# Mixture-of-experts rows stored with their weights applied and added by accumulating gathers, float16 routing tables, and statistics taken four batches ahead

## The chip, the cores and the metric

The kernel runs on one core of one Trainium2 chip. It is written instruction by instruction for five engines: TensorE (PE, matmuls and, beside them, PEld, its weight loads), VectorE (DVE), ScalarE (ACT), GpSimd (POOL) and SyncE (SP, which here only issues DMAs). Engines meet through semaphores. The metric is the device time of one execution in microseconds (us).

## The reference

```python
def _L0_ffn_ref(x, gate_w, w1, b1, w2, b2):        # EMBED_DIM 256, HIDDEN 1024, 8 experts, TOP_K 2
    xt = x.reshape(-1, EMBED_DIM)
    probs = jax.nn.softmax(xt @ gate_w.T, axis=-1)
    top_w, top_i = jax.lax.top_k(probs, TOP_K)
    top_w = top_w / (top_w.sum(axis=-1, keepdims=True) + 1e-09)
    h = jnp.einsum('td,ndh->tnh', xt, w1) + b1
    h = jax.nn.gelu(h, approximate=False)
    out_all = jnp.einsum('tnh,nhd->tnd', h, w2) + b2
    sel = jnp.take_along_axis(out_all, top_i[:, :, None], axis=1)
    return (sel * top_w[:, :, None]).sum(axis=1)

def _L1_attn_ref(x, ...):
    xa = _ln(x, ln1_g, ln1_b)
    xx = _shift(xa)                                # one step back along the sequence
    xk, xv, xr = (xa * m + xx * (1 - m) for m in (time_mix_k, time_mix_v, time_mix_r))
    k, v, r = xk @ att_Wk.T, xv @ att_Wv.T, xr @ att_Wr.T
    x = x + (jax.nn.sigmoid(r) * _wkv(time_decay, time_first, k, v)) @ att_Wo.T
    xc = _ln(x, ln2_g, ln2_b)
    xx2 = _shift(xc)
    xk2, xr2 = (xc * m + xx2 * (1 - m) for m in (cm_k, cm_r))
    kk = jnp.square(jax.nn.relu(xk2 @ ffn_Wk.T))
    return x + jax.nn.sigmoid(xr2 @ ffn_Wr.T) * (kk @ ffn_Wv.T)

# x (16, 256, 256) float32
x = x + decay_attention(_layernorm(x))
x = x + causal_attention(_layernorm(x), ctx_1024)
x = x + _L0_ffn_ref(_layernorm(x))
x = x + _L1_attn_ref(_layernorm(x))
x = x + biased_attention(_layernorm(x), ctx_1024)
x = x + float8_linear(_layernorm(x))
```

## The kernel before

The residual `X` stays in SBUF as 32 tiles of 128 tokens by 256 values from the first step to the last. A batch is one sequence, two tiles; `turns` runs a loop body for the 16 batches. `build` calls one function for each of the six steps. The change is in two of them, `experts_ffn` and `time_channel_mix`.

**Gate stretch of `experts_ffn`.** For each batch VectorE measures mean and variance (`measure`, `layer_norm_stats`), GpSimd takes the inverse root (`inverse_root`), VectorE normalises (`norm`, `layer_norm_apply`) into one of two `XN_s`, SyncE stores these rows to the DRAM table `tokens`, TensorE transposes them (`turn_input`), ScalarE copies them to `xT` (`read_input`), and TensorE multiplies by the gate (`gate_tokens`, 8 matmuls a batch of which each loads 128 token columns and moves 8). There is one `stats`, one `aggr` and one `rstd`; VectorE's turn is norm of batch b+2, measure of batch b+3, copy of the gate's result.

**Routing and tables.** VectorE picks the two largest logits, forms the weights `wt`, counts the tokens of each expert with two matmuls, and gives each pair of token and choice a place in a table of NBLK = 71 blocks of 128 rows, sorted by expert (`place`, `blk`, `row`). The token of each place comes out of TensorE: for each of the 64 columns (two choices, 32 tiles) a one-hot table `at_row` (128 wide) is multiplied by a table `at_blk` (71 wide) that holds the token's number in the column of its block, and all 64 products are summed in `p_y`. The tables are made eight columns at a time, in four buffers:

```python
dve.tensor_tensor(at_row[:, g % 4, :, :], ramp[:, :].unsqueeze(1).broadcast_to([P, 8, P]),
                  flat_row[:, 8 * g:8 * g + 8].unsqueeze(2).broadcast_to([P, 8, P]), ALU.is_equal)
for n in range(8 * g, 8 * g + 8):
    last = dve.tensor_scalar(at_blk[:, g % 4, n % 8, :], ramp[:, 0:NBLK], flat_blk[:, n:n + 1], token[:, n % NT:n % NT + 1],
                             ALU.is_equal, ALU.mult)
```

**Expert loop.** 43 groups, 28 of two blocks and 15 of one. SyncE loads a group's `w1` and `w2` (ring of RING = 4), GpSimd gathers its rows from `tokens` by indirect DMAs (`gx`, four groups ahead), TensorE transposes them, multiplies by `w1` (`p_h`), ScalarE applies gelu, TensorE multiplies by `w2` (`p_y`, which waits for `gy_ready` of the group before), VectorE adds the bias `b2` into `gy`, and ScalarE's queue stores `gy` to the DRAM table `rows_out`. VectorE's `read_rows(j + 1)`, the copy of the next group's transposes, stands before `gy` of group j.

**Mixing stage.** `time_channel_mix` runs 16 turns. GpSimd's `fetch` copies the places of a batch to `which` and gathers four tiles from `rows_out` to `got` (two choices, two tiles), three batches ahead and at the end of its own turn; VectorE's `combine` adds them to `X` with their weights, four dependent products of 256 values, and `measure_x` measures the sum. Then come `roots_x` (GpSimd), `norm_in` (ScalarE), transposes (TensorE, `turn_x`), `xa`, the projections `p_k`, `p_v`, `p_r`, the scans and `mixed_out` on VectorE, and `p_y` on TensorE; the second half takes `zn`, `xc`, `dif`, `mixed2`, the 1024 wide hidden layer `p_h` and `p_kv`. The order on each engine is written out by hand. VectorE's turn has `combine(b + 2)` and `measure_x(b + 2)` between `measured_z` of batch b and `dif` of the channel mix of batch b; TensorE's turn is `p_k` of b+1, `p_y` of b, `p_v` and `p_r` of b+1, values of b-1 around the transposes of `zn`, `turn_x` of b+2, then the receptance and hidden matmuls of b.

## Time and profile before

| what | value |
|---|---|
| median of 3 runs | 2022.05 us (2018.77 to 2024.86) |
| profiled execution, its own time | 2026.54 us |
| its span in the profile | 2024.8 us |
| mean granted clock of TensorE | 0.931 |
| instructions | 40826 |
| PE / PEld busy | 1710.0 us (84%) / 1416.4 us (70%) |
| DVE busy | 1252.0 us (62%) |
| ACT busy | 1121.4 us (55%) |
| POOL busy | 563.3 us (28%) |

The rows below use positions in the span (us from its start). A window's "PEclk" is the granted clock of TensorE, as a share of 2.4 GHz. In the timeline a row is one instruction or a run of equal ones; the square brackets give the idle time of the engine ahead of it and what ended it. The gate stretch lies at 425 to 479 us, routing and tables to 524, the expert loop to about 1043, the mixing stage to about 1545.

### The profile page before, as it was taken

What the parts mean: (1) busy time and instruction counts of PE and PEld (TensorE: products, weight loads), DVE (VectorE), ACT (ScalarE), POOL (GpSimd) and SP (SyncE); (2) the same over time, 40 slices, a digit from 0 to 9 for tenths busy, and PEclk for the clock granted to TensorE, in tenths of its full rate; (3) what the DMA queues carried; (4) which work ended last, traced back from release to release, by engine and by line L of the source; (5) the groups of instructions that cost most, each with busy time, mean ns of one, the idle gap of its engine ahead of it and who ended that gap; (6) DMA issues with size and microseconds to landing.
All of it is one profiled execution on the core that took longest, in us unless ns stands there. A gap on an engine that the chain in (4) does not pass through costs nothing. (4 is left out here: it accounts for less than half of the span.)

```text
span 2024.8 us, 40826 instructions
## 1 busy us (share of the span) xinstructions
PE 1710.0 (84%) x13476; PEld 1416.4 (70%) x13476; DVE 1252.0 (62%) x4322; ACT 1121.4 (55%) x2552; POOL 563.3 (28%) x716
## 2 busy tenths in 40 slices
PE   6677777764699999999955999999978999999964
PEld 5455555554588888889954877777766888888842
DVE  6689999857310101011118899999836988888756
ACT  2299999930122222222325666666636888888855
POOL 3333232221211111101115566666520000000017
PEclk9899999965799999999987999999998999999985
DMA  3100000023556555557940000000010000000002
GB/s 115 46 25 24 19 25 18 2 74 115 169 165 202 174 189 183 180 187 247 326 145 13 20 22 22 22 22 22 11 37 15 23 23 23 23 23 23 2 1 84
DMA packets 102049, 154.68 MB, mean 76 GB/s; under 512 B 5760, under 2 KB 85504, under 8 KB 101088
## 3 DMA queue, kind: packets, MB, share of 16 engines
q1 hardware_dynamic: 85600, 125.25, 18.9%
q0 software_dynamic: 6480, 17.70, 2.9%
q10 hardware_dynamic: 9776, 9.31, 1.3%
q8 instruction: 102, 1.67, 0.3%
q14 instruction: 91, 0.75, 0.1%
HBM read 134.54 MB, written 17.69 MB: 75 GB/s over the span
## 5 line engine op out<-in xcount | busy, mean ns | idle before, releaser
L1851 ACT ACTIVATE moe_hT<-moe_p_h,lane_a 128x256 f32<-128x256 f32 (+1 forms) x344 | 131.5, 433 | 370.5 <-PE moe_p_h L1803 370.4
L1803 PE MATMUL moe_p_h<-moe_gT,moe_w 128*128 128x256 f32 (+1 forms) x1376 | 256.3, 345 | 0.8 <-issue 0.8
L1813 PE MATMUL moe_p_y<-moe_w,moe_hT 128*128 128x256 f32 x1136 | 252.3, 379 | 0.0
L1803 PEld LDWEIGHTS moe_p_h<-moe_gT,moe_w 128*128 128x128 f32 x1376 | 227.8, 192 | 25.7 <-issue 1.2
L1362 ACT ACTIVATE xb_pr<-xb_sc,xb_nmax 128x256 f32<-128x256 f32 x512 | 225.3, 502 | 16.6 <-DVE xb_nmax L1441 16.5
L1813 PEld LDWEIGHTS moe_p_y<-moe_w,moe_hT 128*128 128x128 f32 x1136 | 212.5, 190 | 27.1
L1441 DVE CUSTOM_DVE_ANT_0 xb_sc<-xb_p_s,xb_neg 128x256 f32<-128x256 f32 x512 | 187.2, 420 | 54.5 <-PE xb_p_s L1204 48.2
L852 ACT ACTIVATE xa_pr<-xa_sc,xa_nmax 128x256 f32<-128x256 f32 (+1 forms) x512 | 204.7, 456 | 3.4 <-DVE xa_nmax L934 2.8
L1728 POOL DMA_INDIRECT moe_gx<-moe_tokens,moe_source_i x71 | 67.4, 949 | 460.6 <-PE moe_p_t L1790 400.8
L1981 DVE COPY moe_gT<-moe_p_t 128x512 f32<-128x512 f32 (+1 forms) x43 | 25.7, 598 | 234.7 <-PE moe_p_t L1790 234.7
L1992 DVE TENSOR_TENSOR moe_gy<-moe_p_y,lane_a 128x256 f32<-128x256 f32 x71 | 27.5, 421 | 229.1 <-PE moe_p_y L1813 229.1
L934 DVE CUSTOM_DVE_ANT_0 xa_sc<-xa_p_s,xa_neg 128x256 f32<-128x256 f32 (+1 forms) x512 | 151.7, 352 | 15.3 <-PE xa_p_s L674 13.4
L1216 PE MATMUL xb_p_p<-ident,xb_pr 128*128 128x128 f32 x1024 | 133.9, 274 | 6.1 <-DVE xb_prT L1450 6.1
L686 PE MATMUL xa_p_p<-ident,xa_pr 128*128 128x128 f32 x768 | 118.3, 278 | 14.7 <-DVE xa_prT L943 7.1
L1216 PEld LDWEIGHTS xb_p_p<-ident,xb_pr 128*128 128x128 f32 x1024 | 118.3, 142 | 14.3 <-ACT xb_pr L1362 5.7
L2244 PE MATMUL mix_p_kv<-mix_fv,mix_hid_sq 128*128 128x256 f32 x512 | 115.7, 379 | 1.7 <-ACT mix_hid_sq L2408 1.7
L2293 PE MATMUL mix_p_h<-mix_mixed,mix_fk 128*128 128x256 f32 x512 | 113.6, 380 | 0.0
L686 PEld LDWEIGHTS xa_p_p<-ident,xa_pr 128*128 128x128 f32 x768 | 83.7, 142 | 36.2 <-issue 18.4
L2293 PEld LDWEIGHTS mix_p_h<-mix_mixed,mix_fk 128*128 128x128 f32 x512 | 97.8, 191 | 13.5
L2244 PEld LDWEIGHTS mix_p_kv<-mix_fv,mix_hid_sq 128*128 128x128 f32 x512 | 96.0, 190 | 14.5 <-ACT mix_hid_sq L2408 2.1
L1450 DVE COPY xb_prT<-xb_p_p 128x512 f32<-128x512 f32 x128 | 87.6, 684 | 1.7 <-PE xb_p_p L1216 1.7
L1343 ACT ACTIVATE xb_prT<-xb_p_p 128x512 f32<-128x512 f32 x128 | 75.5, 590 | 7.2 <-PE xb_p_p L1216 4.1
(329 smaller groups left out, 3456.4 us busy)
## 6 DMA issues: line engine op xcount, KB each, us to landing
moe_w<-in_L_ffn_w_dram SPq DMA_DIRECT2D x86, 1024.0 KB
moe_rows_out<-moe_gy ACTq DMA_DIRECT2D x28, 256.0 KB
X<-in_x_dram SPq DMA_DIRECT2D x4, 1024.0 KB, 9.5
xa_ctx<-in_ctx_dram SPq DMA_DIRECT2D x16, 256.0 KB, 3.4
moe_tokens<-moe_XN_s SPq DMA_DIRECT2D x16, 256.0 KB, 2.1
xb_ctx<-in_ctx_dram SPq DMA_DIRECT2D x16, 256.0 KB, 2.9
xb_raw<-in_fside_BxSxS_dram SPq DMA_DIRECT2D x16, 256.0 KB, 3.7
out_dram<-X SPq DMA_DIRECT2D x2, 1280.0 KB, 5.2
```

Of the source, the lines that this page charges most:

```text
L686: last = pe.transpose(p_p[m % 2][:, (e * TB + kt) * P:(e * TB + kt + 1) * P], pr[:, m % RB, e, kt * P:(kt + 1) * P], ident[:, :])
L852: last = act.activation(pr[:, n % RB, e, 0:width], sc[:, n % RB, e, 0:width], ACT.Exp, bias=nmax[:, n % RB, e:e + 1], scale=-1.0)
L934: last = dve.tensor_tensor_reduce(out=sc[:, n % RB, e, 0:keys(t)], in0=scored_in(n, e), in1=neg[:, s, t, 0:keys(t)], scale=1.0, scalar=3e3 ...
L1216: last = pe.transpose(p_p[m % 2][:, (e * TB + kt) * P:(e * TB + kt + 1) * P], pr[:, m % RB, e, kt * P:(kt + 1) * P], ident[:, :])
L1362: last = act.activation(pr[:, n % RB, e, :], sc[:, n % RB, e, :], ACT.Exp, bias=nmax[:, n % RB, e:e + 1], scale=-1.0)
L1441: last = dve.tensor_tensor_reduce(out=sc[:, n % RB, e, :], in0=scored_in(n, e), in1=neg[:, s, t, :], scale=1.0, scalar=3e38, op0=ALU.add, ...
L1450: dve.tensor_copy(*turned_unit(m)).then_inc(s_["p_copied_v"], 1)
L1803: last = pe.matmul(p_h[n % 3][:, k * width:(k + 1) * width], w1[:, r, ic, (2 * n + k) * P:(2 * n + k + 1) * P], gT[:, r % 2, ic, 0:width], ...
L1813: last = pe.matmul(p_y[:, t * D:(t + 1) * D], hT[:, hc, t * P:(t + 1) * P], w2[:, r, hc, :], start=(hc == 0), stop=(hc == HC - 1))
L1851: last = act.activation(hT[:, 2 * n + k, 0:width], p_h[n % 3][:, k * width:(k + 1) * width], ACT.Gelu, bias=b1[:, bass.ds(e * HC + 2 * n + ...
L2244: last = pe.matmul(p_kv[:, t * D:(t + 1) * D], hid_sq[:, hc, t * P:(t + 1) * P], fv[:, hc, :], start=(hc == 0), stop=(hc == HC - 1))
L2293: last = pe.matmul(p_h[m % 2][:, k * S:(k + 1) * S], fk[:, ic, (2 * m + k) * P:(2 * m + k + 1) * P], mixed2[:, 0, ic, :], start=(ic == 0), ...
```

## The change

The statistics get a second set (`stats`, `aggr`, `rstd`) and are taken four batches ahead, behind the copy of the gate's result. TensorE gets `keep_busy(2)` twice a turn in the gate stretch: matmuls of a constant bfloat16 tile into a PSUM bank that is free then. The tables are compared in float16 from float16 copies, `at_blk` for eight columns in one instruction and then multiplied by the token's number in another; the two choices come out in separate halves of `p_y`, so that the choice of a place is known too. The weights' arithmetic moves behind the first `read_rows`; SyncE stores the weights to a DRAM table as 8192 single floats, GpSimd gathers one float per row for each group (`draw_weights`), and VectorE scales the bias and then stores `p_y * weight + b2 * weight`. In the mixing stage `which`, `got` and `combine` are gone: gathers with an adding DMA write straight into `X`, the first choice's four batches ahead, the second's three ahead after the first's have landed, and `measure_x` waits for the second's.

```diff
+                if isinstance(j, int) and j == RING - 1:
+                    sp.wait_ge(s_["weights_ready"], 1)
+                    with nc.allow_non_contiguous_dma(reason="one weight per token and choice"):
+                        sp.dma_start(weights.rearrange("(k t p) a -> p (k t a)", k=2, p=P), wt[:, :, :].rearrange("p k t -> p (k t)")).then_inc(s_["loaded_back"], 16)
...
+            pool.memset(warm[:, :], 1.0).then_inc(s_["warm_set"], 1)
+
+            def norm_root(n, s):
+                wait_alone(pool, s_["stood_p"], (s_["measured"], n + 1))
+                inverse_root(pool, rstd[:, s, :], aggr[:, s, :, 1], 1.0, LN_EPS, minus_half[:, :], s_["var_eps"], s_["rstd_ready"], n, s_["stood_p"])
+
+            for n in range(4):
...
             chain.done(pool.tensor_scalar(falling[:, :], ramp[:, 0:E], -1.0, float(E), ALU.mult, ALU.add))
             chain.done(pool.tensor_scalar(steps[:, :], ramp[:, 0:MAXB], float(P), None, ALU.mult))
             chain.done(pool.tensor_scalar(token[:, :], token[:, :], -float(MID), None, ALU.add))
+            chain.done(pool.tensor_copy(ramp_h[:, :], ramp[:, :]))
+            chain.wait()
+            chain.done(pool.tensor_scalar(token_up[:, :], token[:, :], 0.0, None, ALU.is_ge))
...
-                    wait_alone(pool, s_["stood_p"], (s_["measured"], b + 4))
-                    inverse_root(pool, rstd[:, :], aggr[:, :, 1], 1.0, LN_EPS, minus_half[:, :], s_["var_eps"], s_["rstd_ready"], b + 3, s_["stood_p"])
+                if has_next(b, 4):
+                    norm_root(b + 4, s)
...
+            def draw_weights(j):
+
+                if j >= RING:
+                    pool.wait_ge(s_["gy_ready"], j - RING + 1)
+                for t in range(tiles(j)):
+                    n = first_row(j) // P + t
+                    pool.indirect_dma_start(weight[:, j % RING, t:t + 1], None, weights,
+                                            bass.IndirectOffsetOnAxis(ap=weight_i[:, n:n + 1], axis=0)).then_inc(weighed[j % RING], 16)
...
+                if j == RING - 1:
+                    pool.wait_ge(s_["places_ready"], 1)
+                    pool.wait_ge(s_["loaded_back"], 16)
+                    for i in range(RING):
+                        draw_weights(i)
+                elif j >= RING:
+                    draw_weights(j)
...
+            def keep_busy(n):
+
+                for _ in range(n):
+                    pe.matmul(p_c[:, :], warm[:, 0:P], warm[:, :], start=True, stop=True)
...
             for b, h, s in turns(pe, ahead=3):
                 if has_next(b, 2):
                     turn_input(b + 2, s)
+                keep_busy(2)
                 if has_next(b):
                     gate_tokens(b + 1, 1 - s)
+                keep_busy(2)
...
+                    k, at = divmod(8 * g + n, NT)
+                    last = pe.matmul(p_y[:, k * NBLK:(k + 1) * NBLK], at_row[:, g % 4, n, :], at_blk[:, g % 4, n, :],
+                                     start=(at == 0), stop=(at == NT - 1))
...
-            measure(2)
+            measure(2, 0)
+            measure(3, 1)
...
             for b, h, s in turns(dve, ahead=3):
                 if has_next(b, 2):
                     norm(b + 2, s, h + 1)
-                if has_next(b, 3):
-                    measure(b + 3)
                 dve.wait_ge(s_["logits"], b + 1)
                 dve.tensor_copy(lg[:, bass.ds(TB * b, TB), :], p_h[s][:, 0:TB * E].rearrange("p (t e) -> p t e", t=TB)).then_inc(s_["lg_read"], 1)
+                if has_next(b, 4):
+                    measure(b + 4, s)
...
-            flat_row, flat_blk = flat(row[:, :, :]), flat(blk[:, :, :])
+            chain.done(dve.tensor_copy(blk_h[:, :], flat(blk[:, :, :])))
+            step(dve.tensor_copy(row_h[:, :], flat(row[:, :, :])))
             for g in range(2 * NT // 8):
+                own = slice(8 * g, 8 * g + 8)
+                of = slice(8 * g % NT, 8 * g % NT + 8)
                 if g >= 4:
                     dve.wait_ge(s_["hot_read"], g - 3)
-                dve.tensor_tensor(at_row[:, g % 4, :, :], ramp[:, :].unsqueeze(1).broadcast_to([P, 8, P]),
-                                  flat_row[:, 8 * g:8 * g + 8].unsqueeze(2).broadcast_to([P, 8, P]), ALU.is_equal)
-                for n in range(8 * g, 8 * g + 8):
-                    last = dve.tensor_scalar(at_blk[:, g % 4, n % 8, :], ramp[:, 0:NBLK], flat_blk[:, n:n + 1], token[:, n % NT:n % NT + 1],
-                                             ALU.is_equal, ALU.mult)
-                last.then_inc(s_["hot"], 1)
-            chain.done(dve.tensor_copy(place_i[:, :, :], place[:, :, :]))
-            dve.wait_ge(s_["hot_read"], 2 * NT // 8)
-            dve.tensor_scalar(source_i[:, :], p_y[:, 0:NBLK], float(MID), None, ALU.add).then_inc(s_["source_ready"], 1)
-            chain.close()
-
+                chain.done(dve.tensor_tensor(at_blk[:, g % 4, :, :], ramp_h[:, 0:NBLK].unsqueeze(1).broadcast_to([P, 8, NBLK]),
+                                             blk_h[:, own].unsqueeze(2).broadcast_to([P, 8, NBLK]), ALU.is_equal))
+                chain.done(dve.tensor_tensor(at_row[:, g % 4, :, :], ramp_h[:, :].unsqueeze(1).broadcast_to([P, 8, P]),
+                                             row_h[:, own].unsqueeze(2).broadcast_to([P, 8, P]), ALU.is_equal))
+                chain.wait()
+                dve.tensor_tensor(at_blk[:, g % 4, :, :], at_blk[:, g % 4, :, :],
+                                  token_h[:, of].unsqueeze(2).broadcast_to([P, 8, NBLK]), ALU.mult).then_inc(s_["hot"], 1)
...
+            dve.wait_ge(s_["hot_read"], 2 * NT // 8)
+            step(dve.tensor_copy(codes[:, :, :], p_y[:, 0:2 * NBLK].rearrange("p (k n) -> p k n", k=2)))
+            step(dve.tensor_tensor(code[:, :], codes[:, 0, :], codes[:, 1, :], ALU.add))
+            step(dve.tensor_scalar(code_up[:, :], code[:, :], 0.0, -1.0, ALU.is_gt, ALU.mult))
+            step(dve.scalar_tensor_tensor(source[:, :], code[:, :], float(MID), code_up[:, :], ALU.add, ALU.add))
+            dve.tensor_copy(source_i[:, :], source[:, :]).then_inc(s_["source_ready"], 1)
+            step(dve.tensor_scalar(code_up[:, :], codes[:, 1, :], 0.0, float(B * S), ALU.not_equal, ALU.mult))
+            dve.tensor_tensor(weight_i[:, :], source[:, :], code_up[:, :], ALU.add).then_inc(s_["places_ready"], 1)
             read_rows(0, 0)
+            dve.wait_ge(s_["exp_ready"], 1)
+            step(dve.tensor_reduce(zsum[:, :], probs[:, :, :], AX.X, ALU.add))
+            step(dve.reciprocal(wt[:, 0, :], zsum[:, :]))
+            step(dve.tensor_tensor(wt[:, 1, :], gap[:, :], wt[:, 0, :], ALU.mult))
+            step(dve.tensor_tensor(wsum[:, :], wt[:, 0, :], wt[:, 1, :], ALU.add))
+            step(dve.tensor_scalar(wsum[:, :], wsum[:, :], 1e-9, None, ALU.add))
+            step(dve.reciprocal(wsum[:, :], wsum[:, :]))
+            for k in range(2):
+                chain.done(dve.tensor_tensor(wt[:, k, :], wt[:, k, :], wsum[:, :], ALU.mult))
+            chain.done(dve.tensor_copy(place_i[:, :, :], place[:, :, :]))
+            chain.wait()
+            dve.sem_inc(s_["weights_ready"], 1)
+            chain.close()
+
             for j, r, i in groups(dve):
                 e = expert_of(dve, j)
                 if not isinstance(j, int) or j < NG - 1:
                     read_rows(j + 1, (r + 1) % RING)
+                dve.wait_ge(weighed[r], drawn_by(j, r, i))
+                for t in range(tiles(j)):
+                    last = dve.tensor_scalar(b2_w[:, r % 2, t, :], b2[:, bass.ds(e, 1), :].rearrange("p a d -> p (a d)"), weight[:, r, t:t + 1], None, ALU.mult)
+                last.then_inc(s_["bias_ready"], 1)
+                dve.wait_ge(s_["bias_ready"], j + 1)
...
-                    last = dve.tensor_tensor(gy[:, r % 2, t, :], p_y[:, t * D:(t + 1) * D], b2[:, bass.ds(e, 1), :].rearrange("p a d -> p (a d)"), ALU.add)
+                    last = dve.scalar_tensor_tensor(gy[:, r % 2, t, :], p_y[:, t * D:(t + 1) * D], weight[:, r, t:t + 1], b2_w[:, r % 2, t, :], ALU.mult, ALU.add)
...
-            def fetch(n, s):
-
-                if since(n, 2):
-                    wait_alone(pool, s_["stood_p"], (s_["combined"], n - 1))
-                pool.tensor_copy(which[:, s, :, :], place_i[:, :, bass.ds(TB * n, TB)]).then_inc(s_["which_ready"], 1)
-                wait_alone(pool, s_["stood_p"], (s_["which_ready"], n + 1))
-                for k in range(2):
-                    for t in range(TB):
-                        pool.indirect_dma_start(got[:, s, k, t, :], None, rows_out,
-                                                bass.IndirectOffsetOnAxis(ap=which[:, s, k, t:t + 1], axis=0)).then_inc(fetched[s], 16)
+            def fetch(n, k):
+
+                if k == 1:
+                    pool.wait_ge(fetched[0][n % 2], 32 * (n // 2) + 32)
+                for t in range(TB):
+                    pool.indirect_dma_start(tile_of(X, n, t), None, rows_out,
+                                            bass.IndirectOffsetOnAxis(ap=place_i[:, k, TB * n + t:TB * n + t + 1], axis=0),
+                                            compute_op=ALU.add).then_inc(fetched[k][n % 2], 16)
...
-            fetch(1, 1)
+            fetch(1, 0)
...
+            fetch(0, 1)
+            fetch(1, 1)
...
             fetch(2, 0)
+            fetch(3, 0)
+            fetch(2, 1)
...
+                if has_next(b, 4):
+                    fetch(b + 4, 0)
                 if has_next(b, 3):
-                    fetch(b + 3, 1 - s)
+                    fetch(b + 3, 1)
...
-                dve.wait_ge(fetched[s], 64 * h + 64)
-                for k in range(2):
-                    for t in range(TB):
-                        last = dve.scalar_tensor_tensor(tile_of(X, n, t), got[:, s, k, t, :], wt[:, k, bass.ds(TB * n + t, 1)],
-                                                        tile_of(X, n, t), ALU.mult, ALU.add)
...
             def measure_x(n):
+                dve.wait_ge(fetched[1][n % 2], 32 * (n // 2) + 32)
```

## Rows read from the trace of the kernel before

**Rows 1.** windows: PE, PEld, DVE, ACT, POOL busy (x instructions), PEclk, DMA share, GB/s
```profile
50.00:60.00 10.00, 8.48 (x52) 7.30 (x51) 9.21 (x27) 2.71 (x6) 4.45 (x9) 1.00 0.00 1
...
425.00:479.00 54.00, 42.11 (x192) 40.33 (x192) 27.47 (x111) 9.55 (x16) 16.50 (x44) 0.50 0.30 103
...
550.00:1000.00 450.00, 450.00 (x2302) 400.69 (x2301) 46.47 (x99) 113.91 (x292) 54.79 (x58) 1.00 0.62 204
...
1130.00:1430.00 300.00, 274.64 (x1284) 232.71 (x1284) 277.15 (x484) 187.99 (x356) 192.58 (x184) 1.00 0.07 20
```
**Rows 2.** timeline of the gate stretch: start, us busy, engine, line, group [idle before, releaser]
```profile
440.83 0.73 DVE L91 TENSOR_SCALAR moe_XN_s<-X,moe_aggr,moe_rstd 128x256 f32<-128x256 f32 x2 [1.24 <-POOL moe_rstd L85]
...
441.62 0.71 PEld L1744 LDWEIGHTS moe_p_t<-ident,moe_XN_s 128*128 128x128 f32 x4 [0.45 <-DVE moe_XN_s L91]
...
442.32 1.83 PEld L1753 LDWEIGHTS moe_p_h<-lane_a,moe_xT 128*128 128x128 f32 x8
...
443.81 0.73 DVE L91 TENSOR_SCALAR moe_XN_s<-X,moe_aggr,moe_rstd 128x256 f32<-128x256 f32 x2 [1.24 <-POOL moe_rstd L85]
```
**Rows 3.** timeline of two earlier stages, at clock 1.00
```profile
60.98 0.97 PEld L304 LDWEIGHTS dec_p_m<-dec_ones,dec_osq 128*128 128x128 f32 x8 [0.97 <-DVE dec_o L379]
...
113.75 0.60 PE L640 MATMUL xa_p_a<-lane_b,xa_cT 128*128 128x256 bf16 x4
```
**Rows 4.** groups of instructions by form, whole run: busy, mean ns | idle before
```profile
L640 PE MATMUL xa_p_a<-lane_b,xa_oT 128*128 128x256 bf16 x64 | 9.8, 275 | 11.4 <-ACT xa_oT L800 11.4
...
L965 DVE TENSOR_TENSOR xa_y_f<-xa_y_r,xa_rows_d 128x256 bf16<-128x256 bf16 x32 | 7.9, 288 | 10.4 <-ACT xa_y_r L824 10.3
```
**Rows 5.** timeline of the routing and the tables
```profile
485.75 1.06 PE L1769 MATMUL moe_p_t<-moe_both,moe_ones 128*128 128x256 f32 x2
...
487.88 0.42 DVE L1927 COPY moe_total<-moe_p_t 128x256 f32<-128x256 f32 x1
...
507.86 1.22 DVE L1967 TENSOR_TENSOR moe_at_row<-moe_ramp,moe_row 128x1024 f16<-128x1024 f32 x1
...
510.81 1.22 DVE L1967 TENSOR_TENSOR moe_at_row<-moe_ramp,moe_row 128x1024 f16<-128x1024 f32 x1
```
**Rows 6.** timeline of the expert loop's first groups
```profile
529.45 0.69 DVE L1981 COPY moe_gT<-moe_p_t 128x512 f32<-128x512 f32 x1 [5.81 <-PE moe_p_t L1790]
...
546.84 5.34 PE L1803 MATMUL moe_p_h<-moe_gT,moe_w 128*128 128x256 f32 x24
```
**Rows 7.** parts 3 and 6 of the page: queues, and one of the DMA issues
```profile
q1 hardware_dynamic: 85600, 125.25, 18.9%
...
q10 hardware_dynamic: 9776, 9.31, 1.3%
...
moe_tokens<-moe_XN_s SPq DMA_DIRECT2D x16, 256.0 KB, 2.1
```
**Rows 8.** timeline of one full turn of the mixing stage
```profile
1273.27 1.59 PEld L2232 LDWEIGHTS mix_p_y<-lane_b,mix_mixed_out 128*128 128x128 f32 x8 [1.32 <-DVE mix_mixed_out L2512]
...
1275.59 0.94 POOL L2156 DMA_INDIRECT mix_got<-moe_rows_out,mix_which  x1 [0.30 <-issue]
...
1278.31 2.84 DVE L2431 SCALAR_TENSOR_TENSOR X<-mix_got,wt,X 128x256 f32<-128x256 f32 x4 [0.51 <-DMA mix_got<-moe_rows_out,mix_which]
...
1285.07 0.67 DVE L2552 TENSOR_TENSOR mix_dif<-mix_xc 128x512 f32<-128x512 f32 x1
...
1296.62 1.59 PEld L2220 LDWEIGHTS mix_p_k<-mix_mixed,lane_b 128*128 128x128 f32 x8 [0.26 <-DVE mix_mixed L2423]
...
1299.53 1.59 PEld L2232 LDWEIGHTS mix_p_y<-lane_b,mix_mixed_out 128*128 128x128 f32 x8 [1.32 <-DVE mix_mixed_out L2512]
```
**Rows 9.** timeline of turn 14 of the mixing stage
```profile
1457.39 1.59 PEld L2232 LDWEIGHTS mix_p_y<-lane_b,mix_mixed_out 128*128 128x128 f32 x8 [1.32 <-DVE mix_mixed_out L2512]
...
1467.82 0.69 DVE L2552 TENSOR_TENSOR mix_dif<-mix_xc 128x512 f32<-128x512 f32 x1 [1.51 <-ACT mix_xc L2388]
```
**Rows 10.** timeline of the mixing stage's head
```profile
1055.38 1.80 DVE L2431 SCALAR_TENSOR_TENSOR X<-mix_got,wt,X 128x256 f32<-128x256 f32 x4 [10.11 <-DMA mix_got<-moe_rows_out,mix_which]
```

77 lines of the change are left out of this document (37 added, 40 removed).

## The prediction

> **What bounds the kernel now.** I read the stages first (busy time by window), then the timeline of each stage that the diff touches, then the queues. Four stretches matter, and each has another limit.
>
> In the gate stretch (425 to 479 us) the granted clock of TensorE is 0.50, its 1.2 GHz level [rows 1], and no engine is full. The reader is to see the loop in [rows 2]: `layer_norm_apply` starts at 440.83 and its next turn at 443.81, after 1.24 us of idle that GpSimd's root ends. One batch takes 2.97 us because normalise, measure and root share one `aggr` and one `rstd` and follow each other. VectorE itself has 27.47/16 = 1.72 us of work a batch [rows 1], TensorE 0.71 us of transposes and 1.83 us of gate loads [rows 2].
>
> From 479 to 523.65 us VectorE runs one chain of small steps. The one-hot tables take eight turns of 510.81 - 507.86 = 2.95 us, 23.6 us in all [rows 5].
>
> In the expert loop (550 to 1000) TensorE is busy 450.00 of 450.00 us at clock 1.00 [rows 1]. What the other engines do there costs nothing unless TensorE must wait for it.
>
> In the mixing stage VectorE has 277.15 of 300 us [rows 1]. One turn, from one `p_y` load to the next, is 1299.53 - 1273.27 = 26.26 us [rows 8], and TensorE waits in it: 0.26 us before `p_k` for VectorE's mix and 1.32 us before `p_y` for `mixed_out`. VectorE's wait in the turn is 0.51 us for the gathered rows, before `combine`, which then takes 2.84 us; everything from the first lost half microsecond on is one block of about 3.4 us.
>
> **The change, part by part.**
>
> *Gate stretch.* `measure` now runs four batches ahead with two copies of `aggr` and `rstd`, so the root leaves the loop. VectorE's turn falls to about 1.85 us (its 1.72 and the gaps). TensorE gets four warm matmuls of 512 bf16 columns a batch. A 256-column one costs (0.60 - 0.275)/3 = 0.108 us at the 2.4 GHz level [rows 3, 4], so four of 512 cost 8 x 0.108 = 0.87 us, and 1.73 us at 1.2 GHz. At 2.4 GHz eight loads of 128 columns with hardly any moving columns take 0.97 us [rows 3]; the transposes lie between half of 0.71 and 0.71, I take 0.54. A batch is then 0.54 + 0.97 + 0.87 = 2.4 us at the high level and 0.71 + 1.83 + 1.73 = 4.27 us at the low one. TensorE becomes the limit either way. Which level? Before, TensorE was busy with short loads and stayed at 0.50 [rows 1]. The first stage of the kernel has transposes and matmuls in bursts with gaps, at TensorE busy 8.48 of 10 us, and holds 1.00 [rows 1]; the new loop has no gaps, so I take the high level from the third turn on. The norm at 440.83 is the fifth batch's, so the third's is at 434.9 and the last's at 473.5. These 13 turns take 38.6 us now; with two cold and eleven warm ones they take 8.5 + 26.4 = 34.9: -3.7. Behind the last norm 5.5 us remain until the stretch ends at 479; at the high level transposes, copy, gates and warm matmuls there take about 3.2: -2.3. And the third norm starts some 2 us sooner, since three measurements and roots are done ahead of it. Together -8.0 us; one or three cold turns make it -10 or -6. The `warm` memset lies on GpSimd ahead of the first measurement, the two more set-up copies and two more adds behind the fourth root; both are done long before the fifth root is needed, so nothing. The token stores on SP's queue keep their order.
>
> *Tables.* Per group of eight columns, one 1024-wide compare and eight 71-wide instructions become one 568-wide compare, the 1024-wide one, a wait, and a 568-wide multiply. At one element a cycle, which is what 1.22 us for 1024 says, 568 elements take 0.59 + 0.075 us when the next instruction follows at once and the waited-on compare 1.26: 0.67 + 1.26 + 0.67 = 2.60 us. Eight groups: 20.8 against 23.6, -2.8 us. Two float16 copies of 64 columns add 0.3. Behind the last matmul one write of 71 columns becomes five steps (copy of 142 columns, add, compare, add, cast) of about 0.25 us, as small steps go beside the 0.42 for 256 columns at 487.88 [rows 5]: +1.0. The weights' arithmetic moves away, but the counts land at 485.75 + 1.06 = 486.8 and the copy that needs them starts at 487.88 [rows 5], so only -1.0 of it was on the path. Sum -2.5 us. If float16 ran two elements a cycle the group would be 0.37 + 0.72 + 0.37 = 1.46 us and the tables -11.9; a dense bfloat16 add nearly does, 0.288 us for 256 columns [rows 4]. I take one a cycle: no row has a 16-bit operand that repeats one element. The Trainium skill speaks here against the gain: "Vector Engine (DVE) Microarchitecture Reference", § 5.1, gives the paired mode only to operands that step by one element and reports one repeated element at the single rate, and every compare and multiply here has such an operand. By that rule -2.8 stands, by the dense row -11.9.
>
> *Weights out and back.* SP waits for `weights_ready` behind the fourth load, stores 8192 single floats at a stride of 128, and GpSimd waits for the landing before it draws four groups of weights; behind that wait stand the fifth gather of rows (TensorE wants it four groups of 14 us later) and, on VectorE, `gy` of group 0. The arithmetic sits in front of `read_rows(1)`, where VectorE idles, behind the copy that starts at 529.45 [rows 6]; with its 0.69 and 2.7 for ten small steps it ends at 532.8. Landing after T us, two draws of 1.25 each and 1.8 until they land (1276.54 to 1278.31, [rows 8]), then bias and `gy` 1.6: done at 538.7 + T. TensorE wants `gy` of group 0 when `p_y` of group 1 begins: 24 of its 32 hidden matmuls take 5.34 us from 546.84 on, all 32 take 7.1, and four transposes follow, 0.6 at this clock: 554.5 [rows 6]. So T up to 16 us is free and every further microsecond stalls TensorE. No row has 4-byte writes. Bounds: a whole 256 KB token store lands in 2.1 us [rows 7]; by the mean packet of queue q10 (1.3% of 16 x 2024.8 us over 9776 packets = 43 ns for 0.95 KB) 8192 of them on 16 engines take 22 us, by q1's 71.5 ns for 1.46 KB 37 us [rows 7]. I take 19, just under q10, whose packet is the smaller: +3, bounds 0 and +21. The Trainium skill has a price by "VectorE: DVE Perf Modes", § The three transpose paths: a strided DMA transpose takes 19 times 1309 ns; for half of its 16,384 elements that is, as an estimate, 12.4 us, by which this term would be 0.
>
> In the rest of that loop each pair of tiles adds two draws (2.5 us on GpSimd) and two bias products (0.8 us on VectorE) to engines that are idle most of 14 us; `gy` stays one instruction a tile. Without cover it would be 3.3 us a group; with TensorE at 450 of 450 it is nothing.
>
> *Mixing stage.* `combine` and `which` go; four accumulating gathers a turn replace four plain ones. VectorE's block of 3.4 us does not come back whole. Turn 14 has no `combine` and shows what is late next: there `dif2` starts 1467.82 - 1457.39 = 10.43 us after `p_y`, behind 1.51 us of idle for `xc` [rows 9], against 1285.07 - 1273.27 = 11.80 in a full turn [rows 8]. So VectorE's loop shrinks by 1.37: 10.43 + (1299.53 - 1285.07 = 14.46) = 24.89 us. TensorE's own loop is 26.26 - 1.32 - 0.26 = 24.68: its waits for `zn` and `yn` hang on ScalarE, behind the same `xc`, and stay. The turn is 24.9 us. GpSimd sets the third loop. Its four gathers end at 1276.54 (1275.59 + 0.94 [rows 8]) and VectorE is released 1.8 us later, at 1278.31. Without `which` and its 0.82 us wait the rows land at 5.6 us of the turn; VectorE has room until 6.5 before `dif2` slips. An excess e over a plain gather (landing plus four times the issue) is free up to about 1, and from 2 on it sets the turn: two turns are 48.7 + e, 24.35 + e/2 each. Bounds of e: 0, and 5.6 if both issue (0.95 each) and landing (1.8) double, a turn of 27.1. I take e = 2, since an accumulating gather moves the same rows once more: 25.35 by the strict loop, 24.9 if the contended copies on VectorE shrink as in turn 14; I take 25.0, -1.26 a turn. That counts in turns 1 to 13. Turn 0 doesn't wait for `combine`: 0. 13 x 1.26 = -16.4 us.
>
> At the stage's head VectorE waits 10.11 us for four gathers and has 1.80 us of `combine` before it measures [rows 10]. Now two gathers must land before two more are issued: -1.8 for `combine`, -1.2 for `which` and its wait, about +3 for the second round (issue and landing once more): 0, bounds -4 and +3. The stages before 425 and after the mixing stage are untouched.
>
> **Sum.** -8.0 - 2.5 + 3 + 0 - 16.4 = -23.9, about -24 us on the profiled execution's 2026.5 (span 2024.8 and 1.7 around it): 2002.5. That execution is 4.5 us above the median of the runs, 2022.05; against the median I predict 1998 us. Some 0.3% (6 us) is what a measurement of this kernel can tell from no change.
>
> **Rivals.**
> 1. *The float16 tables run at the paired rate:* -9 more, 1989. For: the dense row. Against: the repeated operand. 0.08.
> 2. *The clock stays low in the gate stretch.* Then a turn is 4.27 instead of 2.97: +18 instead of -8, 2024, no change. For: gate loads hardly move columns, and the same stretch sat at 0.50 while 78% busy. 0.12.
> 3. *The single-float store is slow,* as by q1: +21 instead of +3, 2016. For: a packet's time hardly falls with its size between q1 and q10. Against: four bytes are far less than either moves. 0.10.
> 4. *The turn of the mixing stage doesn't shorten,* since another loop binds (ScalarE, or contention that moves with the work): 2014. For: TensorE's own loop is only 1.58 us shorter than the turn now. Against: turn 14 shows every other step going faster. The leaving of `combine` would then do nothing. 0.10.
> 5. *Slower: the accumulating gathers.* For: two of a batch's gathers wait for the other two. Against: the rows land at 5.6 where 6.5 would do. Place: GpSimd's end of each turn. The rest gives -7.5, so the turn must be above 26.26 + 13.5/13 = 27.3, e above 5.9, or 1 us more issue each and 2 us of landing. With e = 9 a turn is 28.85: +34 - 7.5, 2048. 0.07.
> My forecast: 0.53, own range 1988 to 2009.
>
> The cases between 2016 and 2028 are most of 2 and half of 3; above lie 5 and what is left of 2. Faster 0.77, same 0.13, slower 0.10. For 8 in 10 the range runs from the paired rate with small gains, 1980, to 2020.
>
> **What the profile will show.** Gate stretch: clock 1.00 from about 440 and a turn of 2.4 us, or 0.50 and 4.3. Tables: 568-wide instructions of 0.75 us, a group at 2.6. `gy` of group 0 before 554 less the 10 us gained, and no TensorE gap there. Mixing: `dif2` waits for `xc` in every turn, `p_y` to `p_y` 24.9 to 25.3, VectorE waiting less than 1.5 us for rows. Wrong would be my forecast above all if accumulating gathers hold GpSimd longer than 0.95 us each, or if the clock doesn't rise.

## The result, and the profile after

The changed kernel takes 2017.28 us (median of 14 executions, 2013.83 to 2024.11) against 2022.16 us for the kernel before (14 executions). The ratio is 0.9977 with a 95% interval of 0.9967 to 0.9986: a gain of 4.6 us where 24 were forecast. Measured once more it was 0.9997 (0.9982 to 1.0011), so the gain is near the bound of what can be told from nothing.

The profiled execution of the changed kernel took 2013.83 us (span 2012.0) and is the fastest of its 14. That matters for every difference below: it is 12.7 us under the profiled execution of before, while the medians are 4.9 us apart. So I put the second profile of the changed kernel (from the control experiment, after_again) beside it. The bounds of the stages are the first or last start of one instruction: first statistics of the gate stretch, last copy of gate results, the write of `source_i`, the last `gy`, the first statistics of `X` in the mixing stage, the first and the last `mixed_out`. All in us.

| stage | before | after | after, second profile | forecast | measured |
|---|---|---|---|---|---|
| up to the gate stretch | 425.5 | 423.3 | 425.3 | 0 | -2.2 / -0.2 |
| gate stretch | 53.5 | 42.1 | 42.1 | -8.0 | -11.4 / -11.4 |
| routing and tables | 44.4 | 41.8 | 41.6 | -2.5 | -2.6 / -2.8 |
| expert loop | 516.8 | 530.2 | 536.1 | +3 | +13.4 / +19.3 |
| head, to the first statistics | 17.1 | 21.8 | 21.4 | 0 | +4.7 / +4.3 |
| from there to the first `mixed_out` | 27.8 | 28.3 | 28.4 | 0 | +0.5 / +0.6 |
| turns of the mixing stage | 393.1 | 380.6 | 381.7 | -16.4 | -12.5 / -11.4 |
| rest | 546.6 | 543.9 | 545.1 | 0 | -2.7 / -1.5 |
| span | 2024.8 | 2012.0 | 2021.7 | -23.9 | -12.8 / -3.1 |

The two stages that the change doesn't touch, the first and the last, differ by up to 2.7 us between these three executions (by 3.4 and 5.4 us over all fourteen profiles of this document), nearly as much as the whole gain of the medians; a changed stage's own difference is what can be read.

**Gate stretch.** Windows of the changed kernel (columns as in [rows 1]):

```profile
430.00:460.00 30.00, 29.27 (x196) 24.36 (x201) 22.43 (x88) 7.35 (x13) 15.97 (x42) 0.88 0.32 106
```

The timeline from the moment at which the clock is up:

```profile
440.89 1.08 PEld L1805 LDWEIGHTS moe_p_h<-lane_a,moe_xT 128*128 128x128 f32 x8
441.07 0.74 DVE L91 TENSOR_SCALAR moe_XN_s<-X,moe_aggr,moe_rstd 128x256 f32<-128x256 f32 x2
...
442.67 0.21 PEld L1812 LDWEIGHTS moe_p_c<-moe_warm 128*128 128x128 bf16 x2
442.78 0.59 PE L1812 MATMUL moe_p_c<-moe_warm 128*128 128x512 bf16 x2
...
443.19 0.74 DVE L91 TENSOR_SCALAR moe_XN_s<-X,moe_aggr,moe_rstd 128x256 f32<-128x256 f32 x2
```

Against [rows 2] the turn is 443.19 - 441.07 = 2.12 us in place of 2.97, the normalising instruction has no idle time ahead of it, and the eight gate loads take 1.08 us in place of 1.83, at granted clock 1.00. One wait for the root is left, once, near the stretch's start; GpSimd's set-up stands before that root, with the four small steps that the change adds to it:

```profile
436.88 0.74 DVE L91 TENSOR_SCALAR moe_XN_s<-X,moe_aggr,moe_rstd 128x256 f32<-128x256 f32 x2 [1.37 <-POOL moe_rstd L85]
```

**Tables.** The timeline of one group:

```profile
489.81 0.74 DVE L2016 TENSOR_TENSOR moe_at_blk<-moe_ramp_h,moe_blk_h 128x568 f16<-128x568 f16 x1
...
490.47 1.22 DVE L2018 TENSOR_TENSOR moe_at_row<-moe_ramp_h,moe_row_h 128x1024 f16<-128x1024 f16 x1
...
491.72 0.75 DVE L2021 TENSOR_TENSOR moe_at_blk<-moe_at_blk,moe_token_h 128x568 f16<-128x568 f16 x1
...
492.39 0.74 DVE L2016 TENSOR_TENSOR moe_at_blk<-moe_ramp_h,moe_blk_h 128x568 f16<-128x568 f16 x1
```

A group takes 492.39 - 489.81 = 2.58 us (2.60 forecast, 2.95 before). The 1024-wide compare costs 1.22 us with float16 inputs as it did with float32 inputs [rows 5].

**The weights, out and back.** The timeline around the second group of the expert loop:

```profile
516.19 0.37 SPq L1714 DMA_DIRECT2D moe_weights<-wt  x1
...
523.88 7.07 PE L1868 MATMUL moe_p_y<-moe_w,moe_hT 128*128 128x256 f32 x32
...
541.03 0.94 POOL L1765 DMA_INDIRECT moe_weight<-moe_weights,moe_weight_i  x1 [23.32 <-DMA moe_weights<-wt]
...
548.07 0.61 DVE L2057 TENSOR_SCALAR moe_b_w<-lane_a,moe_weight 128x256 f32 x2 [23.30 <-DMA moe_weight<-moe_weights,moe_weight_i]
...
548.72 0.88 DVE L2064 SCALAR_TENSOR_TENSOR moe_gy<-moe_p_y,moe_weight,moe_b_w 128x256 f32<-128x256 f32 x2
...
549.65 8.87 PE L1868 MATMUL moe_p_y<-moe_w,moe_hT 128*128 128x256 f32 x32 [11.35 <-DVE moe_gy L2064]
```

This is the main line of the document. SyncE issues the store at 516.19, GpSimd's first draw leaves at 541.03, its row reaches VectorE at 548.07, and TensorE, whose 32 matmuls of the second group wait for `gy` of the first, stands idle for 11.35 us. When it starts its granted clock has fallen to 0.50 (window 545 to 548 us), and the 32 matmuls take 8.87 us and not 7.07 as a group earlier, 1.8 us more. 11.35 + 1.8 = 13.2 of the stage's 13.4 us. The list of DMA issues has the store itself, with its size and the time to landing:

```profile
moe_weights<-wt SPq DMA_DIRECT2D x1, 32.0 KB, 24.1
```

The same view's row for queue q1 shows the pieces, 93808 packets where [rows 7] has 85600; 8192 of the 8208 more are the floats:

```profile
q1 hardware_dynamic: 93808, 125.28, 20.1%
```

In the second profile of the same kernel the landing took 29.3 us and TensorE's gap 15.7 us.

**Mixing stage.** The head (timeline):

```profile
1041.56 1.60 POOL L2223 DMA_INDIRECT X<-moe_rows_out,place_i  x1 [31.20 <-POOLq L144]
...
1047.15 1.53 POOL L2223 DMA_INDIRECT X<-moe_rows_out,place_i  x1 [0.31 <-issue]
...
1053.41 1.54 POOL L2223 DMA_INDIRECT X<-moe_rows_out,place_i  x1 [4.49 <-DMA X<-moe_rows_out,place_i]
...
1059.15 0.75 DVE L2503 BATCH_NORM_STATS2 mix_stats<-X 128x6 f32<-128x256 f32 x2 [16.53 <-DMA X<-moe_rows_out,place_i]
```

VectorE waits 16.53 us where [rows 10] has 10.11 and 1.80 of `combine`. A full turn:

```profile
1269.94 1.59 PEld L2306 LDWEIGHTS mix_p_y<-lane_b,mix_mixed_out 128*128 128x128 f32 x8 [0.51 <-DVE mix_mixed_out L2576]
...
1271.04 1.54 POOL L2223 DMA_INDIRECT X<-moe_rows_out,place_i  x1 [0.30 <-issue]
...
1272.89 1.54 POOL L2223 DMA_INDIRECT X<-moe_rows_out,place_i  x1 [0.30 <-issue]
...
1276.72 0.75 DVE L2503 BATCH_NORM_STATS2 mix_stats<-X 128x6 f32<-128x256 f32 x2 [2.25 <-DMA X<-moe_rows_out,place_i]
...
1280.86 0.67 DVE L2613 TENSOR_TENSOR mix_dif<-mix_xc 128x512 f32<-128x512 f32 x1
...
1289.21 4.66 DVE L2497 SCALAR_TENSOR_TENSOR mix_mixed<-mix_dif,lane_b,mix_xa 128x256 f32<-128x256 f32 x6
1289.53 1.46 POOL L2216 TENSOR_TENSOR X<-X,mix_g 128x512 f32<-128x512 f32 x1
...
1295.27 1.59 PEld L2306 LDWEIGHTS mix_p_y<-lane_b,mix_mixed_out 128*128 128x128 f32 x8 [0.52 <-DVE mix_mixed_out L2576]
```

From `p_y` to `p_y` it is 25.33 us (26.26 in [rows 8]). The wait for rows has grown from 0.51 to 2.25 us, an accumulating gather holds GpSimd for 1.54 us where a plain one took 0.94, and TensorE waits 0.52 us for `mixed_out` where it waited 1.32. `dif` comes 10.92 us after `p_y`; from `dif` to the next `p_y` are 14.41 us.

### The profile page after: what moved, and what is told of

Read it like the earlier page. It is cut to its first block and busy times, and to the rows that moved or that the text cites. A ratio compares the mean times of both kernels' runs of the same rounds, so it can differ in the third digit from the quotient of the medians.

```text
span 2012.0 us, 40950 instructions
## 1 busy us (share of the span) xinstructions
PE 1700.0 (84%) x13535; PEld 1404.7 (70%) x13540; DVE 1240.9 (62%) x4289; ACT 1121.0 (56%) x2552; POOL 649.8 (32%) x776
## 3 DMA queue, kind: packets, MB, share of 16 engines
q1 hardware_dynamic: 93808, 125.28, 20.1%
## 5 line engine op out<-in xcount | busy, mean ns | idle before, releaser
L1868 PE MATMUL moe_p_y<-moe_w,moe_hT 128*128 128x256 f32 x1136 | 254.1, 381 | 11.4 <-DVE moe_gy L2064 11.4
L1858 PEld LDWEIGHTS moe_p_h<-moe_gT,moe_w 128*128 128x128 f32 x1376 | 227.9, 192 | 25.8 <-issue 1.2
L1868 PEld LDWEIGHTS moe_p_y<-moe_w,moe_hT 128*128 128x128 f32 x1136 | 213.8, 191 | 39.1 <-DVE moe_gy L2064 11.6
L1765 POOL DMA_INDIRECT moe_weight<-moe_weights,moe_weight_i x71 | 67.0, 943 | 347.0 <-DVE moe_gy L2064 301.7
L934 DVE CUSTOM_DVE_ANT_0 xa_sc<-xa_p_s,xa_neg 128x256 f32<-128x256 f32 (+1 forms) x512 | 151.7, 352 | 15.3 <-PE xa_p_s L674 13.4
L2064 DVE SCALAR_TENSOR_TENSOR moe_gy<-moe_p_y,moe_weight,moe_b_w 128x256 f32<-128x256 f32 x71 | 31.8, 480 | 204.2 <-issue 129.0
L2223 POOL DMA_INDIRECT X<-moe_rows_out,place_i x64 | 101.2, 1581 | 52.7 <-POOLq L144 31.2
```

Of the source, the lines that this page charges most:

```text
L934: last = dve.tensor_tensor_reduce(out=sc[:, n % RB, e, 0:keys(t)], in0=scored_in(n, e), in1=neg[:, s, t, 0:keys(t)], scale=1.0, scalar=3e3 ...
L1858: last = pe.matmul(p_h[n % 3][:, k * width:(k + 1) * width], w1[:, r, ic, (2 * n + k) * P:(2 * n + k + 1) * P], gT[:, r % 2, ic, 0:width], ...
L1868: last = pe.matmul(p_y[:, t * D:(t + 1) * D], hT[:, hc, t * P:(t + 1) * P], w2[:, r, hc, :], start=(hc == 0), stop=(hc == HC - 1))
L2223: pool.indirect_dma_start(tile_of(X, n, t), None, rows_out, bass.IndirectOffsetOnAxis(ap=place_i[:, k, TB * n + t:TB * n + t + 1], axis=0) ...
```

## The experiments

Twelve kernels ran, the last of them the changed kernel itself. Those whose expectation names the changed kernel are built on it, and their ratios too are to the kernel before, so they are to be held against 0.9977; two ratios whose intervals overlap are not told apart. Because the executions differ as the table shows, I read each one's stage in its profile first and its ratio second.

### Which part of the gate stretch's edit gives the gain

`gate_both` is the kernel before with the statistics and the warm matmuls of the change, and nothing else:

```diff
-            for b in range(3):
-                wait_alone(pool, s_["stood_p"], (s_["measured"], b + 1))
+            pool.memset(warm[:, :], 1.0).then_inc(s_["warm_set"], 1)
+            for n in range(4):
+                norm_root(n, n % 2)
...
+                keep_busy(2)
                 if has_next(b):
                     gate_tokens(b + 1, 1 - s)
+                keep_busy(2)
```

> The kernel before with the gate stretch alone changed: two sets of statistics taken four batches ahead, and the warm matmuls. My theory after reading the two traces: the whole 13.6 us that the gate's last copy comes earlier (479.01 to 465.38) belong to this edit, so the kernel takes 2022 - 13.6 = 2008.5 us, ratio 0.993, with turns of 2.1 us at granted clock 1.00. Rival: part of it is given back later in the stage, because weight loads of the first experts or the routing then wait; then the ratio is above 0.995.

Ratio 0.9947 (0.993 to 0.9964), 2014.28 us: 10.7 us gained. Its gate stretch took 41.9 us, 11.6 less than before, and no later stage is more than 0.8 us longer (expert loop 517.5): nothing is given back. The 13.6 us of the theory had 2.2 us in them by which that execution of the changed kernel reached the stretch earlier. gate_both is faster than the whole change, by intervals that don't overlap.

`gate_ahead` leaves out `warm` and both `keep_busy(2)`:

```diff
-                keep_busy(2)
                 if has_next(b):
                     gate_tokens(b + 1, 1 - s)
-                keep_busy(2)
```

> The kernel before with the statistics four batches ahead, without warm matmuls. Theory A: the clock needs the warm matmuls, so TensorE stays at 0.50 and its own 0.71 + 1.83 us and what it waits for ScalarE's copy set a turn of 2.6 to 2.8 us against 2.97: -3 to -5 us, ratio 0.998. Theory B: losing the root's wait is enough to raise the clock; then turns fall below 2 us and the gain is -14 or more, ratio 0.993.

Ratio 0.9956 (0.9941 to 0.9971), 8.9 us gained, stretch 44.4 us, 9.1 less than before. Neither theory was right: the clock stayed at 0.50, as A said, but the gain was twice to three times what A allowed. That the warm matmuls bring the other 1.8 us of gate_both isn't shown, as the two intervals overlap. Timeline:

```profile
449.39 0.90 PEld L1745 LDWEIGHTS moe_p_t<-ident,moe_XN_s 128*128 128x128 f32 x4
...
450.28 1.83 PEld L1754 LDWEIGHTS moe_p_h<-lane_a,moe_xT 128*128 128x128 f32 x8
...
451.85 0.90 PEld L1745 LDWEIGHTS moe_p_t<-ident,moe_XN_s 128*128 128x128 f32 x4
```

The turn is 2.46 us: TensorE's loads back to back at granted clock 0.50, the 1.2 GHz level, with no wait in them.

`gate_warm` is the kernel before with the warm matmuls and the old statistics:

```diff
+                keep_busy(2)
                 if has_next(b):
                     gate_tokens(b + 1, 1 - s)
+                keep_busy(2)
```

> The kernel before with the warm matmuls, statistics as before. If the 2.97 us loop of measure, root and normalise is what binds, the clock rises but the turn stays near 2.97 us: 0 to -3 us, ratio 0.9985 to 1. If TensorE's low clock was in the loop, the turn falls to about 2.4: -8 us, ratio 0.996.

Ratio 0.9986 (0.9975 to 0.9997), inside the first of the two forecasts, but the stretch itself took 55.1 us in its profile, 1.6 more than before, so the little that the ratio shows isn't shown to come from there. The windows show why the stretch is no shorter (columns as in [rows 1]):

```profile
450.00:455.00 5.00, 4.77 (x21) 4.10 (x22) 1.82 (x7) 0.60 (x1) 1.58 (x3) 0.50 0.23 74
455.00:460.00 5.00, 5.00 (x27) 3.78 (x27) 2.68 (x11) 0.62 (x2) 0.89 (x2) 0.66 0.15 52
460.00:465.00 5.00, 4.95 (x39) 4.27 (x39) 2.83 (x13) 1.77 (x3) 1.53 (x4) 1.00 0.31 107
```

Until the clock rose, at about 458, four matmuls of 512 columns a turn at the low level made turns of 4.1 us out of 2.97. In the ten profiles with both edits the clock rose between 437 and 446 us, and the stretch took 41.7 to 45.7 us accordingly: each turn at the low level costs 2 us more than one at the high level. A window of the changed kernel, and two of second_first, in which it rose last:

```profile
434.00:438.00 4.00, 4.00 (x20) 2.98 (x21) 1.93 (x9) 0.60 (x1) 2.96 (x9) 0.62 0.16 52
```

```profile
442.00:446.00 4.00, 4.00 (x18) 3.10 (x17) 1.78 (x7) 0.60 (x1) 0.93 (x2) 0.50 0.18 60
446.00:450.00 4.00, 3.93 (x31) 3.30 (x31) 2.94 (x13) 0.90 (x2) 0.93 (x2) 1.00 0.31 104
```

### Why the store of the weights is slow

`packed_weights` lays the table out by partition, so that a partition stores its 64 floats in one piece, and gets the place from three more small steps:

```diff
-                        sp.dma_start(weights.rearrange("(k t p) a -> p (k t a)", k=2, p=P), wt[:, :, :].rearrange("p k t -> p (k t)")).then_inc(s_["loaded_back"], 16)
+                        sp.dma_start(weights.rearrange("(p k t) a -> p (k t a)", k=2, p=P), wt[:, :, :].rearrange("p k t -> p (k t)")).then_inc(s_["loaded_back"], 16)
...
-            step(dve.tensor_scalar(code_up[:, :], codes[:, 1, :], 0.0, float(B * S), ALU.not_equal, ALU.mult))
-            dve.tensor_tensor(weight_i[:, :], source[:, :], code_up[:, :], ALU.add)
+            step(dve.tensor_scalar(code_up[:, :], codes[:, 1, :], 0.0, float(NT), ALU.not_equal, ALU.mult))
+            step(dve.scalar_tensor_tensor(code[:, :], source[:, :], float(2 * NT), code_up[:, :], ALU.mult, ALU.add))
+            step(dve.tensor_scalar(code_up[:, :], source[:, :], 1.0 / P, -0.498, ALU.mult, ALU.add))
+            step(dve.tensor_scalar(code_up[:, :], code_up[:, :], ROUND, -ROUND, ALU.add, ALU.add))
+            dve.scalar_tensor_tensor(weight_i[:, :], code_up[:, :], 1.0 - 2 * NT * P, code[:, :], ALU.mult, ALU.add)
```

> The changed kernel with the table of weights laid out by partition: each partition stores its 64 floats as one piece of 256 bytes, and three more small VectorE steps work out the place. Theory: the 24.8 us from the store's issue to the first draw are 8192 pieces of 4 bytes, so they fall to 2 or 3 us, TensorE's 11.4 us gap before the second group's second matmuls and the 1.8 us of low clock behind it go: -13 us against the changed kernel, about 2004 us, ratio 0.991. Rival: the store waits for the expert weights' loads on the same queue; then the landing stays near 24 us whatever the pieces' size, and the ratio stays 0.998. Second rival: the draws, which land 7 us after their issue, hold VectorE anyway; then about half of the gap stays.

Ratio 0.9884 (0.9864 to 0.9903), 2002.05 us. The DMA issue and the timeline:

```profile
moe_weights<-wt SPq DMA_DIRECT2D x1, 32.0 KB, 2.3
```

```profile
521.03 0.34 SPq L1714 DMA_DIRECT2D moe_weights<-wt  x1
...
524.08 0.95 POOL L1765 DMA_INDIRECT moe_weight<-moe_weights,moe_weight_i  x1 [1.49 <-DMA moe_weights<-wt]
...
535.58 0.88 DVE L2067 SCALAR_TENSOR_TENSOR moe_gy<-moe_p_y,moe_weight,moe_b_w 128x256 f32<-128x256 f32 x2 [5.78 <-PE moe_p_y L1868]
```

The same 32 KB on the same queue behind the same loads land in 2.3 us. `gy` waits for TensorE and no longer the other way round, and the expert loop takes 516.5 us as before. The rival (waiting behind the experts' loads) and the second rival (the draws) fall. The edit changes the number of the pieces and their addresses together (64 neighbouring floats a partition for floats 128 apart); no run parts the two. Against the changed kernel the ratio is about 19 us better, more than the 13.4 of its fastest execution's profile and near the 19.3 of the second: the landing of the 8192 pieces took 23.9 to 29.3 us in the six profiles that have it, and the loop 529.9 to 536.1 us.

### What sets the turn of the mixing stage

`second_first` swaps two issues at the end of GpSimd's turn:

```diff
+                if has_next(b, 3):
+                    fetch(b + 3, 1)
                 if has_next(b, 4):
                     fetch(b + 4, 0)
-                if has_next(b, 3):
-                    fetch(b + 3, 1)
```

> The changed kernel with the order of two issues on GpSimd swapped in the mixing stage: the second choice's gathers of batch b+3 ahead of the first choice's of b+4. Theory: in the changed kernel a turn is 25.34 us because the second choice's rows land 2.25 us after VectorE has begun to wait; they are issued 3.7 us sooner here, the wait goes, and the turn falls to 24.7 to 24.9, where TensorE's own work or ScalarE's copy xc binds: -0.5 us in 12 turns, -6 us against the changed kernel. Rival: the turn is held by something that only looks like the wait (ScalarE or shared ports); then the idle time moves elsewhere and the turn stays within 0.1 of 25.34.

Ratio 0.998 (0.9971 to 0.999). My theory fell. The wait for rows is gone from VectorE, as meant, and the turn is 25.34 us all the same:

```profile
1275.46 1.59 PEld L2306 LDWEIGHTS mix_p_y<-lane_b,mix_mixed_out 128*128 128x128 f32 x8 [0.53 <-DVE mix_mixed_out L2576]
...
1279.90 0.74 DVE L2503 BATCH_NORM_STATS2 mix_stats<-X 128x6 f32<-128x256 f32 x2
...
1285.89 0.69 DVE L2613 TENSOR_TENSOR mix_dif<-mix_xc 128x512 f32<-128x512 f32 x1 [1.03 <-ACT mix_xc L2462]
...
1294.66 4.73 DVE L2497 SCALAR_TENSOR_TENSOR mix_mixed<-mix_dif,lane_b,mix_xa 128x256 f32<-128x256 f32 x6
1295.05 1.46 POOL L2216 TENSOR_TENSOR X<-X,mix_g 128x512 f32<-128x512 f32 x1
...
1300.81 1.59 PEld L2306 LDWEIGHTS mix_p_y<-lane_b,mix_mixed_out 128*128 128x128 f32 x8 [0.53 <-DVE mix_mixed_out L2576]
```

So the accumulating gathers, dear as they are, did not hold the turn: `dif` starts 10.43 us after `p_y`, as in [rows 9], and the next `p_y` follows 14.92 us later. What is long is this second half of VectorE's turn. Its six products for the time mix take 4.73 us, and GpSimd's two additions to `X` lie beside them. In the kernel before they took 3.48 us:

```profile
1294.66 3.48 DVE L2423 SCALAR_TENSOR_TENSOR mix_mixed<-mix_dif,lane_b,mix_xa 128x256 f32<-128x256 f32 x6
```

The groups of instructions from 1130 to 1430 us, first of the kernel before and then of the changed one, give the mean of one product:

```profile
L2423 DVE SCALAR_TENSOR_TENSOR mix_mixed<-mix_dif,lane_b,mix_xa 128x256 f32<-128x256 f32 x72 | 42.0, 647 | 0.0
```

```profile
L2497 DVE SCALAR_TENSOR_TENSOR mix_mixed<-mix_dif,lane_b,mix_xa 128x256 f32<-128x256 f32 x72 | 56.7, 851 | 0.0
```

`gathers_first` has the swap of `second_first` and also moves GpSimd's two additions behind the gathers:

```diff
-                if not first(b):
-                    add_g(b - 1)
-                if not ended(b):
-                    add_y(b)
                 if has_next(b, 3):
                     fetch(b + 3, 1)
                 if has_next(b, 4):
                     fetch(b + 4, 0)
+                if not first(b):
+                    add_g(b - 1)
+                if not ended(b):
+                    add_y(b)
```

> The kernel of second_first with one more move on GpSimd: its two additions to X (512 columns each, two inputs) stand behind the four gathers instead of ahead of them. With the rows early the turn stayed at 25.34 us, so the wait for them was not what held it. Theory: VectorE's six products for the time mix now run beside these two additions and take 4.7 us instead of 3.5, which is where the rest of the expected gain went. Here they run beside gathers, which only issue: 3.5 us again, and the turn falls to 24.3 to 24.8 us, -6 to -10 us. Rival A: the additions then meet VectorE's adds of Y and the statistics 3 us later and only move the loss: turn 25.2 to 25.5. Rival B: the products' time depends on the gathers' traffic, not on the additions: then they stay at 4.7 us.

The same group in gathers_first, in the same window:

```profile
L2497 DVE SCALAR_TENSOR_TENSOR mix_mixed<-mix_dif,lane_b,mix_xa 128x256 f32<-128x256 f32 x72 | 32.3, 513 | 0.0
```

851 ns (853 in second_first) fell to 513, the six to 2.70 us, beside gathers instead of additions: rival B is out. The turn, from `p_y` to `p_y`, became 24.95 us:

```profile
1250.17 1.70 PEld L2306 LDWEIGHTS mix_p_y<-lane_b,mix_mixed_out 128*128 128x128 f32 x8
...
1275.11 1.70 PEld L2306 LDWEIGHTS mix_p_y<-lane_b,mix_mixed_out 128*128 128x128 f32 x8
```

That is neither the 24.3 to 24.8 of the theory nor the 25.2 to 25.5 of rival A. `p_y` waits no more for `mixed_out`, and TensorE has only 1.41 us of idle left in the turn, for `yn`; its own loop is longer than I had put it. The turns of the stage took 376.9 us in place of 380.6, 3.7 us less. The ratio, 0.9978 (0.9964 to 0.9992), doesn't show it, and its interval is too wide to: 3.7 us are 0.0018.

`plain_rows` keeps the weighted rows and goes back to plain gathers and additions by VectorE:

```diff
+            def combine(n, s, h):
+                dve.wait_ge(fetched[s], 64 * h + 64)
+                for k in range(2):
+                    for t in range(TB):
+                        last = dve.tensor_tensor(tile_of(X, n, t), got[:, s, k, t, :], tile_of(X, n, t), ALU.add)
```

> The changed kernel with the rows still stored weighted, but gathered plainly into a buffer in the mixing stage as before and added to X by VectorE (tensor_tensor in place of scalar_tensor_tensor). Theory: the gain of the mixing turns, 0.9 us each, comes from VectorE being rid of the four additions, so the turn goes back to 26.2 or 26.3 and the head of the stage gets back its shorter 13.9 us; against the changed kernel +12 for the turns, -4.5 for the head: +7 us. Rival: the turn was shortened by something else (the weights' scalar operand, or buffers); then it stays at 25.3. The gathers' issue must fall from 1.55 to 0.95 us each if adding is what makes them dear.

Ratio 1.0003 (0.9991 to 1.0016), 5 us above the changed kernel. Turns are back at 26.1 to 26.5 us (391.5 us for all, against 380.6), the head at 17.1 (against 21.8), a gather's issue between 0.94 and 1.30 us. So the accumulating gathers, with the additions that they take off VectorE, bring 10.9 us in the turns and cost 4.7 in the head.

### The head of the mixing stage

`loads_late` puts one wait ahead of SyncE's three loads:

```diff
+            sp.wait_ge(fetched[1][0], 32)
             sp.dma_start(fk[:, :, :], ins["pack_fk"].rearrange("p (c h) -> p c h", c=DC))
```

> The changed kernel with SyncE's three loads at the head of the mixing stage (3.3 MB) held until the first batch's gathers of the first choice have landed. Theory: these loads are what makes the first gathers land 8 us after their issue and the head 4.5 us longer than before; then the first measurement comes 18.3 us after the stage's start now and at about 12 us here, -6 us, unless fk and fv come too late for the hidden layer. Rival: two rounds of gathers with 1.55 us issues are by themselves 12 to 13 us long, and little moves: under 2 us.

The wait in the kernel is for the second choice's gathers of the first batch, not the first choice's, so the loads left even later than the expectation says, at 1057.89 us. The head took 18.0 us against 21.8 and nothing later waited (28.3 us to the first `mixed_out`, as in the changed kernel): -3.8 us, between theory and rival. Ratio 0.9954 (0.9936 to 0.9972), which overlaps that of the changed kernel, so only the stage shows it. The loads explain most of the 4.7 us; with 18.0 the head is within a microsecond of the 17.1 of before.

### Together

`all_three` has the edits of packed_weights, second_first and loads_late.

> The changed kernel with the table of weights laid out by partition, the second choice's gathers issued first, and the three loads held at the stage's head. If the parts are independent: -13 (weights), -6 (order), -6 to 0 (head) against the changed kernel's 2017: 1992 to 1998 us, ratio 0.985 to 0.988. If the head's loads matter the other way (fk or fv late), 2003.

Ratio 0.987 (0.9853 to 0.9886), 1997.38 us: 27 us under the kernel before. The parts add up except the swap, which by itself was worth nothing.

`all_four` adds the move of gathers_first.

> The kernel of all_three (weights by partition, second choice's gathers first, loads held) with GpSimd's two additions behind the gathers. By the theory of gathers_first 1997.4 - 6 to 10 = 1988 to 1991 us, ratio 0.983; by rival A 1997, ratio 0.987.

Ratio 0.9864 (0.9841 to 0.9886), 1996.32 us. Its turns took 377.7 us (380.6 in all_three) but its gate stretch 45.7 (42.3). The two can't be told apart by their times.

`four_no_warm` takes both `keep_busy(2)` out of it.

> The kernel of all_four without the warm matmuls in the gate stretch (statistics still four batches ahead). With them the stretch took 41.7 to 45.7 us from execution to execution, as the granted clock rose earlier or later; without them (gate_ahead) 44.4 us. Theory: the warm matmuls are worth nothing to 2 us on average: ratio 0.986 to 0.988, the stretch 44.4 us, and the spread of the times narrower. Rival: they also raise the clock of what follows (routing, first experts), then 3 us or more are lost, ratio 0.989.

Ratio 0.9868 (0.9841 to 0.9896), 1994.69 us: the warm matmuls are worth nothing that can be measured. The granted clock was 0.50 from 430 to 470 us. The stretch took 45.7 us, not the 44.4 of gate_ahead, because of one wait of TensorE, which is 0.47 us long there:

```profile
438.06 0.71 PEld L1796 LDWEIGHTS moe_p_t<-ident,moe_XN_s 128*128 128x128 f32 x4 [1.83 <-DVE moe_XN_s L91]
```

It waits for VectorE, and VectorE for the root behind GpSimd's set-up, which in gate_ahead is four small steps shorter. Whether the times spread less isn't settled: four times lie within 5.7 us (1993.58 to 1999.31) where the four of all_four lie within 7.2; the five of gate_ahead lie within 2.2 us and the six of gate_both within 9.0, but the kernel before, without warm matmuls too, spread over 8.1 us in the 16 times beside those.

`after_again` is the changed kernel itself.

> The changed kernel once more on this chip, as the measure for the other runs: ratio 0.997 to 0.999; the gap of 11 to 12 us before the second group's second matmuls, mixing turns of 25.34 us and a head of 21.5 to 22 us must come back in its trace, while the gate stretch may lie anywhere from 41.7 to 45.7 us.

Ratio 0.9997 (0.9982 to 1.0011), turns of 25.31 to 25.35 us, head 21.4 us, gate stretch 42.1 us. The ratio lies above the 0.997 to 0.999 that I expected, the head 0.1 us under its range, and the gap of TensorE was 15.7 us, outside the 11 to 12 that I expected to come back.

## Why the prediction was right or wrong

The direction was right, as far as 4.6 us can be told from nothing, and the size wrong by a factor of five, 24 us forecast. The steps that failed are the weights' way out and back, put at +3 us and measured at +13.4 and +19.3, then the mixing stage's head, put at 0 and measured at +5, and its turns, 4 to 5 us short of the gain; the gate stretch brought 3.4 us more than its term. By its own steps:

- **Gate stretch, -8.0: -11.4 in two profiles, -7.8 to -11.8 over the ten with both edits.** The likeliest clock came true. The turn was 2.12 us for the 2.4 of the sum. What the prediction had not seen is that the high clock matters little: with the root out of the loop and no warm matmuls a turn at the low clock is 2.46 us (gate_ahead), and 8.9 of the 10.7 us come that way. Rival 2 was priced rightly, 4.27 us a turn at the low level and 4.1 measured, and every execution pays it in two to four turns before the clock rises. Two smaller things were wrong. The turns were laid back from 440.83 at an even 2.97 us, which puts the third norm at 434.9; it is at 433.84 in the trace, because the turn from 433.84 to 437.86 is 4.0 us long, with 2.23 us of wait for the root behind GpSimd's set-up. And the longer set-up is not "done long before the fifth root is needed": that norm still waits 1.37 us. Beside TensorE's long turns at the low level this costs nothing; in four_no_warm it costs 1.3 us.
- **Tables, -2.5: -2.6 and -2.8.** A group took 2.58 us for the 2.60 worked out. The single rate was right and rival 1 is out: float16 inputs gain nothing, 1.22 us for 1024 elements as with float32. By the Trainium skill, "Vector Engine (DVE) Microarchitecture Reference", § 5.1, a two-source operation with 2-byte operands, one of which repeats one element, ran at the single rate, and the trace agrees.
- **Weights out and back, +3: +13.4 and +19.3.** This is the step that failed most. The mechanism was put rightly, with its place (`gy` of group 0 against `p_y` of group 1), and so was the bound, 0 to +21. Three sizes were off. The landing was put at 19 us, below the 22 of q10's packet, though the rows gave no packet under 43 ns; it took 24.1 to 29.3. Group 0's two draws were given 2.5 + 1.8 = 4.3 us from the first issue to the landing, by the gathers of the mixing stage; they took 548.07 - 541.03 = 7.0, while the DMA engines moved 108 to 385 GB/s for gathers and loads that had queued up (windows from 540 to 548 us). In packed_weights, with 0 to 1 GB/s beside them, they took at most 5.1. And TensorE's low clock behind a gap was not counted, 1.8 us. The three are 5.1 + 2.7 + 1.8 = 9.6 of the 10.4 us that the term was short. Rival 3, the slow store, comes nearest and had 0.10, but it is right only in that the store is slow: it wanted 37 us of landing, by q1's packet, and the pieces cost little more than q10's 43 ns. Its reason, that a packet's time hardly falls with its size, misreads [rows 7], where 71.5 to 43 ns for 1.46 to 0.95 KB is a fall in step with the size. That its total of 2016 us is near the measured 2017.28 is luck, since it rests on a head at 0 and turns at -16.4. The 12.4 us of landing estimated from the Trainium skill, "VectorE: DVE Perf Modes", § The three transpose paths, are half of the measured 24.1.
- **Head of the mixing stage, 0: +4.9 to +5.2 with the stretch behind it.** The prediction took 3 us for the second round of gathers. It left out that the first round, for which the second must now wait, runs beside SyncE's three loads; holding these gave 3.8 us back (loads_late).
- **Turns, -16.4: -12.5 and -11.4.** 25.34 us in place of 25.0. The estimate for the accumulating gather, 2 us of excess, was low: four issues of 1.54 for 0.94 are 2.4, the landing 2.3 us (from 1274.43, the end of the last issue, to 1276.72) for 1.8, together 2.9, with which the prediction's strict loop would give 25.8. But this was not what bound, as second_first shows. The loop of VectorE was put together from a row of turn 14 (10.43 us to `dif`) and one of a full turn (14.46 from there on), as if the second would stay. It hardly changed in the changed kernel (14.41), but only because a gain and a loss meet: the products for `xc` and the two steps of `mix_a` became 1.3 us shorter, the six products for `xa` 1.18 us longer (4.66 for 3.48). With `dif` at 10.43 the rest took 14.92 (second_first); 0.31 of the 0.51 us more is one step of `mix_a` (1.47 us for 1.16) that then lies beside a product of GpSimd. That a copy slows beside GpSimd had been in the prediction as a hope, "if the contended copies shrink": the product groups for `xc` did, from 733 to 479 ns, and those for `xa` grew from 647 to 851. So rival 4's "contention that moves with the work" holds in part: the turn shortened by 0.93 us of 1.26. And TensorE's own loop, 24.68 by the prediction, is 24.95 (gathers_first).
- **The price put on the executions.** The sum was made against one execution of 2026.5 us and set 4.5 us lower for the median. The two profiles of the changed kernel, 9.7 us apart, show that one execution's stages can't be carried to the median where a stage has a landing that varies.

The rule of the Trainium skill that bears on the turns is in "SBUF — State Buffer", § Who interferes with whom: a VectorE instruction with two SBUF inputs contends with a GpSimd instruction that reads SBUF. The trace agrees: the products read two tensors in SBUF, and cost 851 ns beside GpSimd's additions and 513 beside the issues of its gathers.

What stays open: why the landing of the 8192 pieces varies between 23.9 and 29.3 us in the same kernel, and when the clock rises in the gate stretch, which differed by some 9 us between executions. That a piece of four bytes costs about as much as one of a kilobyte is an estimate: 24.1 us x 16 engines / 8192 = 47 ns, against 43 ns for q10's packets [rows 7]. The share of queue q1 agrees roughly: over the six profiles with the scattered store it is 1.0 to 1.6 points of 16 engines' span above [rows 7] (19.9 to 20.5% against 18.9%), 39 to 62 ns for each of the 8208 packets more.

## What to carry to other kernels

Count a DMA by its pieces before its bytes: 8192 floats scattered took 24 to 29 us where the same 32 KB in 128 pieces took 2.3, and it ate more than the gate stretch had gained. When work is taken off the busiest engine, don't stitch the new turn from rows of two different turns: everything behind the cut slides against the other engines, and two-input VectorE work that now lies beside GpSimd's costs up to 1.7 times as much. Take a dependent step out of a loop before warming a clock for it: 8.9 of 10.7 us came without the warm matmuls. These cost 1.6 us in every turn until the clock has risen (4.1 for 2.46) and give back 0.34 in every turn behind it (2.12 for 2.46); in a loop of 16 turns no pair of runs here tells what is left from nothing.

## What the runs showed of the hardware that was not expected

- An accumulating indirect gather of 128 rows of 1 KB held GpSimd for 1.55 us (median of 64, 1.53 to 1.95), a plain one for 0.95 (0.94 to 1.30).
- The scattered store's landing took 23.9, 24.0, 24.1, 26.2, 26.3 and 29.3 us in six executions, and 2.3 us packed.
- A compare of 1024 elements with one operand that repeats each element cost VectorE 1.22 us with float16 and with float32 inputs.
- With the same instructions in the stretch, and TensorE busy for 3.78 to 4.00 us of every 4 us from 430 us on, the granted clock rose from 0.50 to 1.00 at about 437 us in one execution (the changed kernel) and at about 446 in another (second_first).
